# A second, turned load of the tokens, normalised in place by VectorE, in a decoder layer

## The reference

```
def _layernorm(x, axis=-1, eps=1e-05):
    m = jnp.mean(x, axis=axis, keepdims=True)
    v = jnp.var(x, axis=axis, keepdims=True)
    return (x - m) / jnp.sqrt(v + eps)

x = x + self_attention(_layernorm(x), w_q, w_k, w_v, w_o)       # 32 heads of 16
x = x + cross_attention(_layernorm(x), ctx, ctx, positions, mask, Wq, Wk, Wv, Wo)  # 32 query heads, 8 key heads of 128
x = x + linear_with_loras(_layernorm(x), ...)
```

## Time and profile before

| | |
|---|---|
| median of 3 runs | 1413.53 us (1412.81 to 1415.68) |
| profiled execution | 1413.3 us |
| span from first to last instruction | 1411.1 us |
| busy: TensorE, VectorE, ScalarE, GpSimd | 98%, 72%, 31%, 37% of the span |
| mean granted TensorE clock | 0.996 of full speed |

### The profile page before, as it was taken

How to read it: one execution, slowest core, us unless ns; L and a number is a source line. 1 busy time by engine, 2 the same in 40 slices (tenths; PEclk the granted TensorE clock), 3 DMA queues, 4 the chain that set the end, 5 groups by cost and what they waited for, 6 DMA issues and landing times.

```text
span 1411.1 us, 27857 instructions
## 1 busy us (share of the span) xinstructions
PE 1379.6 (98%) x11552; PEld 1146.4 (81%) x11552; DVE 1021.5 (72%) x1476; ACT 440.7 (31%) x751; POOL 529.2 (37%) x457
## 2 busy tenths in 40 slices
PE   8999999999997799999999999999999999999999
PEld 6888888788886688888888888888888888888787
DVE  3755553788989977767767767777777777778765
ACT  5311233666657442122122122113123122122432
POOL 4422310444344524344344344344344344342131
PEclk9999999999999999999999999999999999999999
DMA  8654220000005012012011012011011011002011
GB/s 268 218 180 148 99 89 1 18 3 25 10 3 166 16 34 73 16 46 61 16 46 60 16 46 60 16 46 54 22 46 48 28 46 46 31 16 89 30 53 67
DMA packets 78859, 83.03 MB, mean 59 GB/s; under 512 B 9824, under 2 KB 50928, under 8 KB 78480
## 3 DMA queue, kind: packets, MB, share of 16 engines
q1 hardware_dynamic: 68832, 63.16, 14.3%
q10 hardware_dynamic: 9360, 17.04, 3.9%
q0 software_dynamic: 544, 1.06, 0.3%
HBM read 58.17 MB, written 23.07 MB: 58 GB/s over the span
## 4 chain that ended last, share of the span: by engine, by line
PE 60%; POOL 3%; DVE 1%; ACT 0%; issue 0%; ACTq 0%
PE p_ps_y L1272 6%; PE p_ps_y L1273 6%; PE p_ps_y L1274 6%; PE p_ps_qk L75 4%; PE p_ps_s L1233 3%; PE p_ps_qk L77 3%; PE p_ps_qk L76 3%; POOL p_wo_lo L1196 3%; PE p_ps_s L1244 2%; PE p_ps_s L1272 2%; PE p_ps_s L1274 2%; PE p_ps_s L1273 2%; PE p_ps_o L76 2%; PE p_ps_o L75 2%; PE p_ps_s L75 2%; PE p_ps_o L77 2%
## 5 line engine op out<-in xcount | busy, mean ns | idle before, releaser
L1650 POOL TENSOR_TENSOR p_q_rot<-p_q_rot,p_rb 128x512 f32<-128x512 f32 x128 | 167.2, 1306 | 310.7 <-DVE p_rb L171 310.7
L1272 PE MATMUL p_ps_y<-p_wo_hi,p_o_hi 128*128 128x512 f32 x384 | 151.2, 394 | 2.0 <-DVE p_o_lo L1526 1.3
L1273 PE MATMUL p_ps_y<-p_wo_lo,p_o_hi 128*128 128x512 f32 x384 | 149.5, 389 | 0.0
L1274 PE MATMUL p_ps_y<-p_wo_hi,p_o_lo 128*128 128x512 f32 x384 | 149.4, 389 | 0.0
L75 PE MATMUL p_ps_qk<-p_xt_hi,p_wq_hi 128*128 128x512 f32 x312 | 126.8, 406 | 0.9 <-DVE p_xt_lo L1550 0.9
L1031 POOL TENSOR_TENSOR p_pn<-p_p,p_inv 128x512 f32<-128x512 f32 x64 | 66.1, 1063 | 154.2 <-DVE p_inv L920 152.0
L1535 DVE TENSOR_TENSOR x_sb<-p_ps_y,x_sb 128x512 f32<-128x512 f32 x96 | 66.4, 692 | 77.0 <-PE p_ps_y L1274 76.0
L77 PE MATMUL p_ps_qk<-p_xt_hi,p_wq_lo 128*128 128x512 f32 x312 | 122.0, 391 | 0.0
L76 PE MATMUL p_ps_qk<-p_xt_lo,p_wq_hi 128*128 128x512 f32 x312 | 121.8, 390 | 0.0
L1380 ACT ACTIVATE p_pt_hi<-p_ps_s 128x512 fp32r<-128x512 f32 x64 | 34.9, 597 | 257.8 <-PE p_ps_s L1244 257.7
L1386 ACT ACTIVATE p_o_hi<-p_ps_s 128x512 fp32r<-128x512 f32 x64 | 34.7, 595 | 230.0 <-PE p_ps_s L1259 230.0
(11 more groups left out here) (262 smaller groups left out, 3774.1 us busy)
## 6 DMA issues: line engine op xcount, KB each, us to landing
k_scratch<-p_k_out SPq DMA_DIRECT2D x32, 256.0 KB, 2.1
p_raw<-in_wq SPq DMA_DIRECT2D x32, 256.0 KB, 3.2
p_raw<-in_wo SPq DMA_DIRECT2D x32, 256.0 KB, 2.7
p_k_t<-k_scratch ACTq DMA_DIRECT2D x32, 256.0 KB, 2.7
p_v_in<-v_scratch ACTq DMA_DIRECT2D x32, 256.0 KB, 2.8
v_scratch<-p_v_out SPq DMA_DIRECT2D x24, 256.0 KB, 2.6
x_sb<-in_x SPq DMA_DIRECT2D x16, 256.0 KB, 3.0
out<-p_y SPq DMA_DIRECT2D x16, 256.0 KB, 2.0
```

The costliest lines, as they stand in the source:

```text
L1272: nc.tensor.matmul(ps_y[t][:, :], oh, w_hi["o"][h][:, :], start=(h == 0), stop=False)
L1273: nc.tensor.matmul(ps_y[t][:, :], oh, w_lo["o"][h][:, :], start=False, stop=False)
L1274: mm = nc.tensor.matmul(ps_y[t][:, :], ol, w_hi["o"][h][:, :], start=False, stop=(h == H - 1))
L1650: nc.gpsimd.tensor_tensor(q_rot[:, h, :], q_rot[:, h, :], rb[:, :], ALU.add).then_inc(q_added, 1)
```

## The change

The host hands in the tokens a second time, turned (`xt`, features by tokens). SP loads them in four pieces of 1 MB, one for each block of tokens, at the start of block 3 into `xt_raw`, which lies where `xt_lo` lies. TensorE turns the mean and the inverse root once (`turn_norm`, two transposes, in front of values (3, 1)); ScalarE copies them (`copy_norm`), SP stores them as two rows of 2,048 numbers in memory (`store_norm`) and loads them back spread over all 128 partitions (`load_rows`): the tables of blocks 0 and 1 behind the stores of head 2 of block 3, those of blocks 2 and 3 behind all stores of keys and values, ahead of the heads table and the q, k and o weights. VectorE subtracts the mean (`centre_tile`) and multiplies by the inverse root (`scale_tile`) in place, and the lo part is made in place as well. `turn_tile` and `normalise_tile` are gone. VectorE runs four to five tiles ahead of `values(t)`; ScalarE's hi parts run three tiles further ahead than before, and the first q, k and o weights are split at t = 5, 6 and 7. To make room, the buffers of `KeysAndValues` move within the same memory.

```
+            def load_turned_tokens():
+                sp.wait_ge(c_ready, NB * KC)
+                sp.wait_ge(ready["k"], KVH)
+                sp.wait_ge(row_turned, NB)
+                for blk in range(NB):
+                    tokens = slice(blk * BLOCK, (blk + 1) * BLOCK)
+                    sp.dma_start(xt_raw[:, :, tokens], xt_dram[:, :, tokens]).then_inc(xt_in if blk == 0 else xt_rest_in, 16)
+            def store_norm():
+                sp.wait_ge(row_copied, NB + 1)
+                for i, scr in enumerate((mean_scr, rstd_scr)):
+                    sp.dma_start(scr.rearrange("o (t p) -> (o t) p", p=P), norm_rows[:, i, :]).then_inc(scr_out, 16)
+            def load_rows(blk, loaded):
+                sp.wait_ge(tables_out, 16 * 2 * NB)
+                sp.wait_ge(scr_out, SCR_OUT)
+                for rows_of, scr in ((mean_rows, mean_scr), (rstd_rows, rstd_scr)):
+                    sp.dma_start(rows_of[blk][:, :], scr[:, blk * BLOCK:(blk + 1) * BLOCK].broadcast_to([P, BLOCK])).then_inc(loaded, 16)
...
+                if b == NB - 1:
+                    load_turned_tokens()
                 for i in range(KVH):
                     store_keys(b, i)
                     store_values(b, i)
+                    if b == NB - 1 and i == 1:
+                        store_norm()
+                    if b == NB - 1 and i == 2:
+                        load_rows(0, near_rows_in)
+                        load_rows(1, near_rows_in)
...
                 sp.wait_ge(v_stored[i], 16 * (NB - 1) * KVH // 2)
+            load_rows(2, far_rows_in)
+            load_rows(3, far_rows_in)
...
+            def copy_norm():
+                act.wait_ge(row_turned, NB + 1)
+                nc.scalar.activation(norm_rows[:, :, :], ps_r[0][0:TILES, 0:2 * P].rearrange("t (i p) -> t i p", i=2), ACT.Copy).then_inc(row_copied, 1)
...
+            def turn_norm():
+                pe.wait_ge(norm1.norm, 1)
+                for i, part in enumerate((norm1.mv[:, :, 0], norm1.rstd[:, :])):
+                    tr = nc.tensor.transpose(ps_r[0][0:TILES, i * P:(i + 1) * P], part, ident[:, :])
+                tr.then_inc(row_turned, 1)
...
                     keys(b, i, (lambda c: need(pe, c_ready, b * KC + c + 1)) if i == 0 else (lambda c: None))
                     extra(b, i)
+                    if b == NB - 1 and i == 1:
+                        turn_norm()
                     values(b, i)
...
-            def turn_tile(t):
-                need(pe, xn_ready, t + 1)
-                need(pe, tile_lo, t - 1)
-                for c in range(KC):
-                    tr = nc.tensor.transpose(ps_t[t % 2][:, c * P:(c + 1) * P], xn[t % 2][:, c * P:(c + 1) * P], ident[:, :])
-                tr.then_inc(transposed, 1)
...
             def tile_parts_hi(t):
-                need(act, transposed, t + 1)
+                need(act, scaled, t + 1)
...
             def beside_values(b, i):
...
-                if b == NB - 1 and i == KVH - 1:
+                if b == NB - 1 and i == KVH - 3:
                     tile_parts_hi(0)
                     tile_parts_hi(1)
+                if b == NB - 1 and i > KVH - 3:
+                    tile_parts_hi(i - KVH + 4)
             kv.scalar(act, beside_values)
             for t in range(1, TILES):
-                if t > 1:
-                    tile_parts_hi(t)
+                if t + 3 < TILES:
+                    tile_parts_hi(t + 3)
                 copy_values(t - 1)
-                if 3 <= t < 6:
-                    split_hi(act, "qko"[t - 3], 0, done["q"], 0)
+                if 5 <= t < 8:
+                    split_hi(act, "qko"[t - 5], 0, done["q"], 0)
...
+            def centre_tile(t):
+                kv.wait_rows(dve, t // TPB)
+                xs, mean = xt_raw[:, :, t * P:(t + 1) * P], mean_rows[t // TPB][:, t % TPB * P:(t % TPB + 1) * P]
+                nc.vector.tensor_tensor(xs, xs, mean.unsqueeze(1).broadcast_to([P, KC, P]), ALU.subtract).then_inc(centred, 1)
+            def scale_tile(t):
+                need(dve, centred, t + 1)
+                xs, scale = xt_raw[:, :, t * P:(t + 1) * P], rstd_rows[t // TPB][:, t % TPB * P:(t % TPB + 1) * P]
+                nc.vector.tensor_tensor(xs, xs, scale.unsqueeze(1).broadcast_to([P, KC, P]), ALU.mult).then_inc(scaled, 1)
...
             def beside_values(b, i):
...
+                if b == NB - 1 and i == KVH - 4:
+                    centre_tile(0)
+                    centre_tile(1)
+                    scale_tile(0)
+                if b == NB - 1 and i == KVH - 3:
+                    scale_tile(1)
+                    centre_tile(2)
                 if b == NB - 1 and i == KVH - 2:
-                    normalise_tile(0)
-                    normalise_tile(1)
+                    tile_parts_lo(0)
+                    scale_tile(2)
+                    centre_tile(3)
+                    tile_parts_lo(1)
+                if b == NB - 1 and i == KVH - 1:
+                    scale_tile(3)
+                    tile_parts_lo(2)
+                    centre_tile(4)
+                    tile_parts_lo(3)
             kv.vector(dve, beside_values)
...
+            centre_tile(TPB + 1)
+            scale_tile(TPB)
             for t in range(TILES):
-                if 0 < t < TILES - 1:
-                    normalise_tile(t + 1)
-                tile_parts_lo(t)
-                if 3 <= t < 6:
-                    split_lo(dve, "qko"[t - 3], 0)
+                if t + TPB + 2 < TILES:
+                    centre_tile(t + TPB + 2)
+                if t + TPB + 1 < TILES:
+                    scale_tile(t + TPB + 1)
+                if t + TPB < TILES:
+                    tile_parts_lo(t + TPB)
+                if 5 <= t < 8:
+                    split_lo(dve, "qko"[t - 5], 0)
```

More of the change, by code:

```diff
@@ L217, in __init__ @@
         v_raw_in = [m.sem(f"p1_v_raw_in{i}") for i in range(KC + 1)]
-        c_in0 = [m.sem(f"p1_c_in0_{c}") for c in range(KC)]
+        c_in0 = [m.sem(f"p1_{n}") for n in ("c_in0_0_and_xt", "c_in0_1_and_xt_rest", "c_in0_2_and_near_rows", "c_in0_3_and_norm_and_far_rows")]
+        xt_in, xt_rest_in, near_rows_in, far_rows_in = c_in0
+        scr_out = far_rows_in
+        XT_IN, XT_REST_IN, NEAR_ROWS_IN, SCR_OUT, FAR_ROWS_IN = 16 + 16, 16 + 16 * (NB - 1), 16 + 16 * 4, 16 + 16 * 2, 16 + 16 * 2 + 16 * 4
         c_in = m.sem("p1_c_in")
@@ L544, in attention @@
         o_hi, o_lo = m.sb("o_hi", [P, BLOCK], F32R), m.sb("o_lo", [P, BLOCK], F32R)
-        xn = [nc.alloc_sbuf_tensor_at(f"p3_xn{i}", [P, HIDDEN], F32, offset=xn_at + 4 * HIDDEN * i) for i in range(2)]
+        xt_raw = nc.alloc_sbuf_tensor_at("p3_xt_raw", [P, KC, TOKENS], F32, offset=base + 32 * 1024)
+        mean_rows, rstd_rows = ([nc.alloc_sbuf_tensor_at(f"p3_{n}_rows{b}", [P, BLOCK], F32, offset=base + at * 1024) for b, at in enumerate(places)]
+                                for n, places in (("mean", (12, 152, 142, 146)), ("rstd", (20, 170, 144, 148))))
         assert xn_at == base + 170 * 1024 and nc.sbuf_base == xn_at + 2 * 4 * HIDDEN
@@ L805, in tile_parts_hi @@
             def tile_parts_hi(t):
[L806 removed]
+                need(act, scaled, t + 1)
                 need(act, kv.wv1_ready, KC)
[L808 removed]
+                need(act, kv.tables_out, 16 * 2 * NB)
+                if t == TPB:
+                    for stored in kv.k_stored[0:2]:
+                        need(act, stored, 16 * NB * KVH // 4)
+                if t == 3 * TPB:
+                    need(act, kv.k_terms, NB * KVH)
+                    need(act, kv.k_added, NB * KVH)
+                nc.scalar.activation(xt_hi[:, :, t * P:(t + 1) * P], xt_raw[:, :, t * P:(t + 1) * P], ACT.Copy).then_inc(tile_hi, 1)
             def copy_values(t):
@@ L1961, in decoder_layer @@
         sin_scr = nc.dram_tensor("sin_scratch", (P, TOKENS), F32, kind="Internal").ap()
+        mean_scr, rstd_scr = (nc.dram_tensor(n + "_scratch", (1, TOKENS), F32, kind="Internal").ap() for n in ("mean", "rstd"))
         xs, ident = m.sb("x_sb", [P, TILES, HIDDEN]), m.sb("ident", [P, P])
```

78 lines of the change are left out of this document (38 added, 40 removed).

## The result

| | before | after |
|---|---|---|
| median of 4 runs | 1413.46 us (1412.81 to 1415.68) | 1430.12 us (1428.05 to 1431.5) |
| span of the profiled execution | 1411.1 us | 1426.0 us |
| mean granted TensorE clock | 0.996 | 0.993 |

The account below looks back on a forecast made before the run. TensorE, busy for 98% of the span, was taken to bound the kernel. Removed transposes 7.8 us, less 0.3 for turn_norm and 1.0 for a stall, save 6.5: 1413.5 to 1407.0 us, range 1404.8 to 1409.8.

Parts of the forecast that it names:

- Behind the stretch: After the changed stretch: all engines arrive earlier by the same amount, the 1.68 us wait stays, nothing comes by the clock.
- three were about waits on data: VectorE in time: 1406.0, chance 0.20; longer stall behind block 3: 1408.0 to 1409.5, 0.18; far tables 1-5 us late: 0.07.
- The rival on the clock: After the 1.68 us wait at 253.4 us: 1.7 us dip gone (1405.3), or another at 190.6 (1408.7); chance 0.10.
- The removed transposes and the norm's two: On TensorE: transposes of 16 turn_tile calls removed save 7.8 us; turn_norm's two added transposes cost 0.3 us.
- no wait was forecast: In front of values (3, 1): rstd done at 149.41 us, TensorE reaches turn_norm at 149.52, so no wait.
- VectorE beside GpSimd: Block 3, heads 4 to 7: the two take turns, one key addition costing VectorE 1.29 us in each head.
- Scale 4: VectorE's scaling of tile 4, behind block 3: ends at 190.3 us, or 188.5 without a lock.
- The stall in front of values(2): Behind block 3 TensorE waits for ScalarE's first copy of own values: 1.0 us, bounds 0 and 2.5.
- The far tables: Norm tables of blocks 2 and 3: land at 195.3, 3.1 us after last issue; no charge, cover 1.9 us.
- the limit of 197.2: Latest harmless landing of the far tables, since TensorE needs the copy of values 3 at about 199.7 us.
- The four loads of 1 MB: Sync queue in block 3, from about 143.6 us: 4.2 MB in 13 us, done at about 158.
- The first value store: Behind the four loads: ScalarE's copy of tile 2 waits until about 158, TensorE needs it from 165.9; 7 us cover.

Follow-up runs that it names:

- experiment 1: The changed kernel with 138 empty instructions on TensorE's queue ahead of its first wait: 1419.09 us, ratio 1.0034.
- 2: The kernel before with 118 empty instructions ahead of TensorE's first wait: 1441.89 us, ratio 1.0203.
- 4: The changed kernel with 256 empty instructions ahead of TensorE's first wait: 1456.15 us, ratio 1.0292.
- 9: The changed kernel with 9 empty instructions in each self-attention iteration from scores(5) on: 1446.6 us, ratio 1.0154.
- 5: The changed kernel with 138 empty instructions spread over blocks 1 to 3 of keys and values: 1416.83 us, ratio 0.9961.

## Why the prediction was wrong

**The step that failed** is "Behind the stretch": "All engines arrive earlier by the same amount." and "Nothing there comes by the clock." They did arrive earlier by 6.3 us, but TensorE's program is 138 instructions shorter at that point, and the self-attention's scores depend on where in the program they stand. That cost 13.0 us in gaps of issue, where TensorE waited for its next block of instructions, and about 5.6 us in the three iterations where the clock fell behind a gap. No rival had it: three were about waits on data in the stretch that the diff touches, one about the clock at waits that were known. Shown by experiments 1, 2, 4 and 9 and by the packets of the instruction queue; that the change is a gain without it, by 5.

The rival on the clock was half right and its price too high. In the changed kernel the dip behind the 1.68 us wait is gone, as it considered, but that was worth 0.45 us (14.83 - 14.38) and not 1.7. In the kernel of experiment 1 the clock is 0.83 again in the 10 us from 260, and scores(1) to scores(2) takes 15.50 us; what decides it no run here shows.

**Point by point, in the stretch.** The removed transposes and the norm's two: 6.5 us were forecast, and 6.3 - 0.4 = 5.9 us had been gained by scores(1). turn_norm's weight load waited 0.2 us for the reciprocal, where no wait was forecast, and still the whole of turn_norm cost 0.24 us instead of 0.3 (the lead over the kernel before falls from 0.41 to 0.17 us across it).

VectorE beside GpSimd was as worked out. VectorE's timeline of the changed kernel, for the earlier trace rows:

```profile
174.24 1.78 DVE L1001 TENSOR_TENSOR p_xt_raw<-p_xt_raw,p_rstd_rows 128x512 f32<-128x512 f32 x1
175.95 0.68 DVE L995 TENSOR_TENSOR p_xt_raw<-p_xt_raw,p_mean_rows 128x512 f32<-128x512 f32 x1
...
188.63 0.68 DVE L1001 TENSOR_TENSOR p_xt_raw<-p_xt_raw,p_rstd_rows 128x512 f32<-128x512 f32 x1
...
197.18 0.69 DVE L995 TENSOR_TENSOR p_xt_raw<-p_xt_raw,p_mean_rows 128x512 f32<-128x512 f32 x1 [4.25 <-DMA p_rstd_rows<-rstd_scratch]
```

An operation beside the key addition takes 1.78 us, 1.1 more than its neighbours at 0.68, and it happens once in each of heads 5, 6 and 7 as forecast (174.24, 179.49 and 185.12). With GpSimd idle, centre and scale take 0.68 us and start 0.60 apart. So an addition cost VectorE 1.1 us and not 1.29. Scale 4 ended at 189.3, not 190.3.

The stall in front of values(2) was forecast at 1.0 us. TensorE's timeline at values(1) and values(2):

```profile
187.43 0.39 PE L75 MATMUL p_ps_qk<-p_wv_hi,p_xt_hi 128*128 128x512 f32 x1
...
190.61 0.47 PE L75 MATMUL p_ps_o<-p_wv_hi,p_xt_hi 128*128 128x512 f32 x1 [0.30 <-ACT p_v L865]
```

The bracket says 0.30 us, but values(2) start 3.18 us behind values(1) instead of 2.72, and their own first matmuls lose another 0.11: the stall cost 0.57 us. The bracket counts from the modelled end of a matmul, so for a stall of TensorE starts are the better measure, as the prediction said of durations.

The far tables, forecast to cost nothing, cost 1.0. They landed by 197.18 and not at 195.3: the queue of SP and then ScalarE's timeline,

```profile
190.86 0.42 SPq L312 DMA_DIRECT2D p_rstd_rows<-rstd_scratch  x1
```

```profile
198.51 0.63 ACT L861 ACTIVATE p_xt_hi<-p_xt_raw 128x512 fp32r<-128x512 f32 x1 [4.25 <-DVE p_xt_raw L1001]
199.04 0.58 ACT L865 ACTIVATE p_v<-p_ps_qk 128x512 f32<-128x512 f32 x1
```

and TensorE's:

```profile
199.77 0.47 PE L75 MATMUL p_ps_qk<-p_wv_hi,p_xt_hi 128*128 128x512 f32 x1 [0.71 <-ACT p_v L865]
```

This is the chain that the prediction traced for the tables: centre 8, scale 7, hi 7, copy of values 3, TensorE. Two numbers in it were off. The landing came 6.3 us behind the last issue instead of 3.1. And the limit of 197.2, which the landing just met, was too late: TensorE was ready for values(5) at 198.9 us (values(2) at 190.61, 0.11 lost, three periods of 2.72), not at 199.7. It started at 199.77, 0.9 us late, and lost 0.1 more behind it.

So the two stalls cost 1.6 us where 1.0 was forecast, and the gain of the stretch adds up. Of the 6.3 us, 0.4 are not the change's; with 0.2 for turn_norm and 1.6 for the stalls put back, the removed transposes make 7.7, where 7.8 was forecast.

The four loads of 1 MB were issued at 143.27 and took 10.0 us each to land (median), within the cover that the prediction had. The first value store behind them held up ScalarE's copy of tile 2 by 5.7 us, until 159.3 us (about 158 forecast); no wait of TensorE ends on a store of block 3.

**Behind it all** 1.8 us of the span lie behind the last scores. Between kernels of this study this part varies in the same way (982 to 984.6 us from the last scores to the end), and with it the clock in the gap around 490 to 520 us; what sets it is not settled.

**What stays open.** Why the packet comes late just there. A block that ends a little behind the edge is all fast matmuls (the end of the mixing, L732 in the changed kernel, and scores, some 1.7 us of work for 256 instructions), but so is one that ends at 160, and it costs nothing: in the kernel before, the packet began 2.4 us ahead of scores(13), with its border at 147 (401.44 and 403.81), and 1.5 us ahead of scores(15), at 165 (427.84 and 429.29). What starts a packet was not tried. Nor is it known why the clock fell behind three of the ten gaps and not behind the others.

## What to carry to other kernels

An edit that only takes instructions away shifts everything behind it in the instruction stream. Where a long row of fast small matmuls follows (here 128 in 1.6 us, load and matmul each an instruction), count the instructions of the program up to it: if the position modulo 256 moves, look for rows with "issue" in the table of waits before judging the edit itself. The packets of the queue of kind "instruction" show whether a gap is the fetching. Undo the shift with empty instructions spread among long ones, and compare again; and don't put them in a row ahead of the first work, where they cost 0.06 to 0.09 us each (4.8 us for 80, 7.1 for 118, 10.3 for 138, 23.5 for 256).

## What the hardware showed that I had not expected

- A border of 256 instructions in the last third of the scores' 128 fast matmuls cost 0.7 to 2.7 us (just behind them 0.4 to 2.3), and the clock can fall behind it: 0.83 over 10 us behind the gaps at 302, 332 and 363 us, and 1.00 over the stretches from 270 to 300 with gaps of the same size in them.
- A block of 256 instructions needed 2.2 to 3.0 us from the start of its packet to the first matmul out of it (72 gaps), while 256 instructions of the scores took 1.5 us.
- The same kernel has a different time on different chips: medians of the kernel before were 1414.05, 1421.82 and 1424.96 us on three.
- A table of 256 KB in which every partition reads the same 2 KB took 6.3 us from the last of four issues to the first use.
